# Routed experts and three convolution layers: VectorE's filter products, row normalisation and two start-up steps in another order

## The chip, the cores and the metric

One core of a Trainium2 chip runs the whole kernel in one launch. The metric is the device time in microseconds (us) of that core. A time is the median of several executions; the profile comes from one execution more.

## What is computed

The input x has 4 batches of 512 tokens with 512 channels (16 heads of 32). Four layers follow, each `x = x + layer(groupnorm(x))`. The first is a mixture of 8 experts with the best 2 per token; the other three are causal depthwise convolutions over the tokens with 3, 7 and 15 taps, mixed by a small matrix. Cut to what matters:

```
logits = x @ gate_w.T                      # groupnorm(x), 2048 tokens x 512
top_logit, top_idx = top_k(logits, 2);  gw = softmax(top_logit)
for e in range(8):
    we = sum(where(top_idx == e, gw, 0))
    out += we * ((silu(x @ w1[e].T) * (x @ w3[e].T)) @ w2[e].T)
...
y = concat([causal_dwconv(x, w) for w in (w3, w7, w15)])   # layers 1 to 3
out = einsum('blhm,dm->blhd', y, w_mix)
```

Everything is float32; a product is made of three passes (high by high, high by low, low by high) over a high part and a low part of each operand.

## The kernel before

The experts part takes about 745 us and the convolutions the rest. Gating and routing come first. Then the tokens stand in 35 blocks of 128 rows, sorted by expert, 4 or 5 blocks to each. For block g of expert e the engines do this:

- **GpSimd (POOL)** gathers the 128 rows of block g+1 from x into `block_row` by an indirect DMA (`fetch_rows`, L429 to L436), once TensorE has turned block g (`xT_done`), and then adds the finished rows of block g-2 into `acc` in DRAM by another (`add_block`, L438 to L446). It waits for that addition to land before it goes on. There is one `block_row`.
- **VectorE (DVE)** normalises the gathered rows (`normalise_rows`, L727), multiplies gate and up (`hidden`, L785), and makes the low parts: of x (`xT_low`, L768), of the turned hidden rows (`hT_low`, L773), of w1 and w3 (L733) and of w2 (L740).
- **ScalarE (ACT)** makes the high parts (w2: L517; hT: L534; filters: L524), SiLU (L552), and takes the finished, weighted rows out of PSUM (`y_row`, L540).
- **TensorE (PE)** runs in `body`: 48 matmuls for gate and up of block g (L934), the turn of block g+1 (`next_rows`, four transposes, L911), the down product of block g-1 (L921, L924), and eight transposes of hidden (L946).
- **SyncE (SP)** loads w1, w3 (`w13_raw`, 4 pieces) and w2 (2 halves) of the next expert as soon as their buffers are free, and then stores this expert's filters (L376), in this order in its queue.

While the experts run, VectorE also builds the block Toeplitz filters of the convolutions, one expert after the other, between the first and the second block of experts 1 to 7 (`after_first`): six products of taps and mixing matrix (L755), of which ScalarE takes the high part (L524) and VectorE the low part (L763). They lie in `filter_sb`, which is a piece of the tile `rows`, and go from there to DRAM. `filter_sb` is cleared once (L453), since the products fill only part of it; `filters_out` counts the stores, and the products of expert e wait until those of expert e-1 have landed.

The order of work on each engine is written out by hand. `all_blocks` (L332) sets it: for an expert, `new_expert`, `body` for its first block, `after_first`, and then `body` for each of the other blocks.

At the start, `place`, `weight_block` and other one-hot matrices of the routing borrow the tiles of w2. `at_block` lies in `w2_raw`, and VectorE's `expand_weights` is the last to read it; TensorE's `find_weights` (L902) reads `place` and `weight_block` in `w2_hi` and `w2_lo` and ends with `values_done`.

Of the kernel before, what the change touches and what calls it, by code (L numbers as in the profile page):

```python
# [11 lines left out]
TOP_K = 2  # L12
# [10 lines left out]
PARTS_OF_WEIGHT = 2  # L23
# [126 lines left out]
def wait_apart(eng, semaphore, value, counter):  # L150

    eng.wait_ge(semaphore, value)
    eng.sem_inc(counter, 1)


def experts_part(nc, x, gate_wT, w13T, w2T, acc, ident, group_mean, taps, mixT, filters, filters_out):
# [5 lines left out]
    with ExitStack() as ctx:  # L162
# [6 lines left out]
        def sem(name):  # L169
            return ctx.enter_context(nc.semaphore(name))  # L170
# [28 lines left out]
        filter_sb = late_rows[:, 0:4 * LAGS].rearrange("p (i s n) -> p i s n", i=2, s=2)  # L199
# [80 lines left out]
        weight_block_ok = sem("weight_block_ok")  # L280
        ids_done = sem("ids_done")
        lanes_done = sem("lanes_done")
        values_done = sem("values_done")
# [28 lines left out]
        filter_zero = sem("filter_zero")  # L312
# [6 lines left out]
        def load_w13(eng, e, k):  # L319
            eng.dma_start(w13_raw[:, k], w13T[bass.ds(e, 1), k].rearrange("o p t n -> (o p) t n"))\  # L320
               .then_inc(w13_in[k], 16)

        def load_w2(eng, e, half):
            k = slice(half * KF // 2, (half + 1) * KF // 2)
            eng.dma_start(w2_raw[:, k], w2T[bass.ds(e, 1), :, k].rearrange("o p t n -> (o p) t n"))\
               .then_inc(w2_in[half], 16)

        def last_block_of(eng, e):

            return eng.value_load(table[0:1, bass.ds(e, 1)], min_val=0, max_val=MAX_BLOCKS - 1)  # L330
# [17 lines left out]
        @block.sync  # L348
        def _(sp):
            for b in range(BATCH):  # L350
                sp.dma_start(rows[:, b * QUARTERS:(b + 1) * QUARTERS, 0:D], x_rows[b]).then_inc(x_in[b], 16)
            for k in range(KD):
                load_w13(sp, 0, k)

            sp.wait_ge(values_done, 1)
            for half in range(2):
                load_w2(sp, 0, half)


            sp.dma_start(taps_sb, taps).then_inc(taps_in, 16)  # L360
            sp.dma_start(mix_sb, mixT).then_inc(taps_in, 16)


            with sp.Fori(1, E) as e:
                for k in range(KD):
                    sp.wait_ge(w13_ok, (e - 1) * KD + k + 1)
                    if k >= 2:
                        sp.wait_ge(w13_in[k - 2], 16 * (e + 1))
                    load_w13(sp, e, k)
                for half in range(2):  # L370
                    sp.wait_ge(w2_ok, (e - 1) * 2 + half + 1)
                    sp.wait_ge(w13_in[KD - 2 + half], 16 * (e + 1))
                    load_w2(sp, e, half)
                for i in range(2):
                    wait_apart(sp, filter_ok, e * 2 + (i - 1), sp_passed)
                    sp.dma_start(filters[:, bass.ds(e * 8 + (4 * i - 8), P // HD)].rearrange("r a s n -> r a (s n)"),  # L376
                                 filter_sb[:, i].rearrange("p s n -> p (s n)")).then_inc(filters_out, 16)

        @block.gpsimd
        def _(pool):  # L380
# [48 lines left out]
            def fetch_rows(g):  # L429

                at = slice(g, g + 1) if isinstance(g, int) else bass.ds(g, 1)
                nc.gpsimd.tensor_copy(fetch[:, :], from_row[:, at]).then_inc(fetch_ok, 1)
                wait_apart(pool, fetch_ok, g + 1, passed)
                pool.indirect_dma_start(
                    out=block_row[:, :], out_offset=None, in_=x_by_row,
                    in_offset=bass.IndirectOffsetOnAxis(fetch[:, 0:1].bitcast(u32), 0)).then_inc(row_in, 16)  # L436
# [10 lines left out]

            pool.wait_ge(route_ok, 1)
            fetch_rows(0)
            pool.wait_ge(xT_done, 1)  # L450
            fetch_rows(1)
            pool.wait_ge(values_ok, 1)
            nc.gpsimd.memset(filter_sb, 0.0).then_inc(filter_zero, 1)  # L453
            pool.wait_ge(acc_ready, 32)
            pool.sem_inc(y_free, FREE)

# [9 lines left out]
            g = last_block_of(pool, E - 1)  # L466
# [100 lines left out]
        def _(dve):  # L567
# [148 lines left out]
            def take_weights():  # L716

                dve.wait_ge(values_done, 1)
                step(nc.vector.tensor_copy(row_value[:, 2, 1:1 + COLUMNS], y_ps[:, 0:COLUMNS]))
                nc.vector.tensor_tensor(row_value[:, 2, 1:1 + COLUMNS], row_value[:, 2, 1:1 + COLUMNS],  # L720
                                        y_ps[:, COLUMNS:2 * COLUMNS], ALU.add).then_inc(values_ok, 1)

            def normalise_rows(g):

                at = slice(g + 1, g + 2) if isinstance(g, int) else bass.ds(g + 1, 1)
                dve.wait_ge(row_in, 16 * (g + 1))
                nc.vector.tensor_scalar(block_row[:, :], block_row[:, :], row_value[:, 0, at], row_value[:, 1, at],  # L727
                                        ALU.subtract, ALU.mult).then_inc(row_ok, 1)
# [7 lines left out]
            def split_w2(e, g0):  # L736
                for half in range(2):
                    dve.wait_ge(w2_hi_ok, 2 * e + (half + 1))
                    k = slice(half * KF // 2, (half + 1) * KF // 2)
                    nc.vector.tensor_tensor(w2_lo[:, k], w2_raw[:, k], w2_hi[:, k].bitcast(f32),  # L740
                                            ALU.subtract).then_inc(w2_ok, 1)

            def after_first(e, g0):
                split_w2(e, g0)
                if isinstance(e, int):
                    dve.wait_ge(taps_in, 32)
                    dve.wait_ge(filter_zero, 1)
                    return
                dve.wait_ge(filters_out, e * 32 + (FILTERS_FREE - 32))
                for i in range(2):  # L750
                    c = bass.ds(e * 2 + (i - 2), 1)
                    tap = 0
                    for s, k in enumerate(SCALES):
                        at = SCALE_AT[s] + (QUARTERS - 1) * HD
                        last = nc.vector.tensor_tensor(  # L755
                            filter_sb[:, i, 1, at:at + k * HD].rearrange("p (k d) -> p k d", d=HD),
                            taps_sb[:, c, tap:tap + k].rearrange("p o k -> p (o k)")[:, :, None].to_broadcast([P, k, HD]),
                            mix_sb[:, c, s, :].to_broadcast([P, k, HD]), ALU.mult)
                        tap += k
                    last.then_inc(product_ok, 1)  # L760
                for i in range(2):
                    dve.wait_ge(filter_hi_ok, e * 2 + (i - 1))
                    nc.vector.tensor_tensor(filter_sb[:, i, 1].bitcast(f32r), filter_sb[:, i, 1], filter_sb[:, i, 0],  # L763
                                            ALU.subtract).then_inc(filter_ok, 1)

            def xT_low(g):
                dve.wait_ge(xT_hi_ok, g + 1)
                nc.vector.tensor_tensor(xT_lo[:, :, :].rearrange("p a n -> p (a n)"), xT_ps[:, :],  # L768
                                        xT_hi[:, :, :].rearrange("p a n -> p (a n)").bitcast(f32), ALU.subtract).then_inc(xT_ok, 1)

            def hT_low(g):
                dve.wait_ge(hT_hi_ok, g + 1)
                nc.vector.tensor_tensor(hT_lo[:, :, :], hT_ps[:, :, :], hT_hi[:, :, :].bitcast(f32),  # L773
                                        ALU.subtract).then_inc(hT_ok, 1)

            def body(e, g, first):
                if not isinstance(g, int):
                    hT_low(g - 1)
                if isinstance(g, int) or not first:
                    normalise_rows(g + 1)  # L780
                dve.wait_ge(silu_ok, g + 1)
                if not isinstance(g, int):

                    dve.wait_ge(hT_done, g)
                nc.vector.tensor_tensor(hidden[:, :].rearrange("p (a n) -> p a n", a=2),  # L785
                                        silu[:, :].rearrange("p (a n) -> p a n", a=2), up_ps[:, :, :],
                                        ALU.mult).then_inc(hidden_ok, 1)
                xT_low(g + 1)
                if isinstance(g, int):
                    take_weights()  # L790
# [15 lines left out]
            expand_weights()  # L806
            take_targets()
            all_blocks(dve, new_expert, body, after_first)
            hT_low(last_block_of(dve, E - 1))

# [684 lines left out]
```

## Time and profile before

| | |
|---|---|
| median of 3 runs | 1171.56 us (1164.51 to 1361.69) |
| profiled execution, device time | 1166.2 us |
| its span | 1164.3 us |
| TensorE matmuls busy | 1060.9 us (91%) |
| VectorE busy | 501.3 us (43%) |
| ScalarE busy | 318.5 us (27%) |
| GpSimd busy | 128.1 us (11%) |
| experts part in the span | 0 to about 745 us |

How to read it: busy shares are averages over stages. TensorE has work nearly all the time, so what matters is where it has none, and what ended each of those gaps. In the timeline a bracket behind a row gives the idle time of the engine ahead of it and the instruction that ended it; "PEclk" is the clock granted to TensorE, as a share of full speed. The device time is 1.9 us longer than the span, for what lies around it.

### The profile page before, as it was taken

Reading aid. Unit: us, or ns where it says so; the run is one execution under the profiler, and the core shown is the slowest. Engines: PE = TensorE matmul, PEld = TensorE weight load, DVE = VectorE, ACT = ScalarE, POOL = GpSimd, SP = SyncE. Lnnn points to the kernel's source line nnn. Section 1 sums busy time; section 2 is a strip of 40 time slices with the busy share of each in tenths; the row PEclk is TensorE's granted clock in tenths of the full one; section 3 lists DMA queues with packets and bytes.
Section 4 is the critical chain, followed back from the end, with each engine's and each line's share of the span. In section 5 each row is a group of like instructions: output and inputs, shape, how many; then the busy total and the mean of one; then the engine's idle time right before and its main releaser. Section 6 shows DMA issues by size and latency. Waiting matters only on the chain. (4 is left out here: it accounts for less than half of the span.)

```text
span 1164.3 us, 14374 instructions
## 1 busy us (share of the span) xinstructions
PE 1060.9 (91%) x5234; PEld 883.5 (76%) x5235; DVE 501.3 (43%) x692; ACT 318.5 (27%) x433; POOL 128.1 (11%) x170
## 2 busy tenths in 40 slices
PE   5588999999999999999999999168999979989998
PEld 3377887887887887887878877158888968888887
DVE  5773163154245263154451452135325952387011
ACT  2403242142243242153431432012301220122112
POOL 2013111211211212111212111000000000000000
PEclk9769999999999999999999999667999989999999
DMA  8208218316415519217338140492998299698993
GB/s 361 82 19 316 48 28 314 76 27 245 138 33 196 185 18 351 39 27 278 105 112 275 27 137 18 128 238 63 205 193 182 47 220 208 127 192 168 204 207 100
DMA packets 66336, 172.72 MB, mean 148 GB/s; under 512 B 8192, under 2 KB 38016, under 8 KB 57280
## 3 DMA queue, kind: packets, MB, share of 16 engines
q1 hardware_dynamic: 58080, 149.19, 45.1%
q0 software_dynamic: 8080, 23.07, 9.4%
q8 instruction: 21, 0.34, 0.1%
q14 instruction: 11, 0.09, 0.0%
q10 hardware_dynamic: 144, 0.02, 0.0%
HBM read 136.15 MB, written 40.30 MB: 152 GB/s over the span
## 5 line engine op out<-in xcount | busy, mean ns | idle before, releaser
L1409 PE MATMUL head_ps<-split,ring 128*128 128x512 f32 (+1 forms) x630 | 225.8, 358 | 18.7 <-DMA ring<-filters 17.2
L1413 PE MATMUL head_ps<-split,ring 128*128 128x512 f32 (+1 forms) x630 | 220.2, 350 | 0.0
L1410 PE MATMUL head_ps<-split,ring 128*128 128x512 f32 (+1 forms) x630 | 219.8, 349 | 0.0
L1409 PEld LDWEIGHTS head_ps<-split,ring 128*128 128x128 f32 x630 | 123.6, 196 | 35.2 <-DMA ring<-filters 17.8
L1413 PEld LDWEIGHTS head_ps<-split,ring 128*128 128x128 f32 x630 | 123.3, 196 | 15.7
L1410 PEld LDWEIGHTS head_ps<-split,ring 128*128 128x128 f32 x630 | 123.7, 196 | 14.9
L921 PE MATMUL y_ps<-w_hi,hT_hi 128*128 128x512 f32 x280 | 117.5, 420 | 1.2 <-ACT hT_hi L534 1.2
L785 DVE TENSOR_TENSOR hidden<-silu,up_ps 128x1024 f32<-128x1024 f32 x35 | 42.7, 1219 | 165.0 <-ACT silu L552 165.0
L921 PE MATMUL y_ps<-w_lo,hT_hi 128*128 128x512 f32 x280 | 113.5, 405 | 0.0
L1236 DVE TENSOR_TENSOR stream<-stream,head_ps 128x512 f32<-128x512 f32 (+1 forms) x63 | 34.1, 557 | 176.2 <-PE head_ps L1413 176.2
L773 DVE TENSOR_TENSOR hT_lo<-hT_ps,hT_hi 128x1024 fp32r<-128x1024 f32 x35 | 42.7, 1221 | 134.0 <-ACT hT_hi L534 134.0
L552 ACT ACTIVATE silu<-gate_ps 128x1024 f32<-128x1024 f32 x35 | 35.9, 1025 | 235.5 <-PE up_ps L934 235.5
L934 PE MATMUL gate_ps<-w_hi,xT_hi 128*128 128x512 f32 x280 | 89.9, 402 | 1.7 <-DVE xT_lo L768 1.7
L443 POOL DMA_INDIRECT acc<-y_row,put x35 | 63.4, 1810 | 214.6 <-ACT y_row L540 206.3
L934 PE MATMUL up_ps<-w_hi,xT_hi 128*128 128x512 f32 x280 | 86.9, 392 | 0.0
L934 PE MATMUL up_ps<-w_lo,xT_hi 128*128 128x512 f32 x280 | 86.8, 391 | 0.0
L934 PE MATMUL gate_ps<-w_lo,xT_hi 128*128 128x512 f32 x280 | 86.7, 391 | 0.0
L934 PE MATMUL gate_ps<-w_hi,xT_lo 128*128 128x512 f32 x280 | 86.6, 391 | 0.0
L934 PE MATMUL up_ps<-w_hi,xT_lo 128*128 128x512 f32 x280 | 86.3, 390 | 0.0
L733 DVE TENSOR_TENSOR w_lo<-w_raw,w_hi 128x2048 fp32r<-128x2048 f32 x32 | 71.9, 2285 | 4.7 <-ACT w_hi L509 4.7
L924 PE MATMUL y_ps<-w_hi,hT_lo 128*128 128x512 f32 x280 | 69.3, 389 | 0.0
L921 PEld LDWEIGHTS y_ps<-w_hi,hT_hi 128*128 128x128 f32 x280 | 55.7, 199 | 12.8 <-issue 1.4
(189 smaller groups left out, 1362.8 us busy)
## 6 DMA issues: line engine op xcount, KB each, us to landing
w_raw<-in_w13T SPq DMA_DIRECT2D x32, 1024.0 KB, 11.5
ring<-filters SPq DMA_DIRECT2D x60, 480.0 KB, 10.4
filters<-rows SPq DMA_DIRECT2D x14, 1568.0 KB, 7.2
w_raw<-in_w2T SPq DMA_DIRECT2D x16, 1024.0 KB, 6.1
ring<-filters SPq DMA_DIRECT2D x84, 192.0 KB, 6.2
ring<-filters SPq DMA_DIRECT2D x48, 288.0 KB, 7.2
rows<-in_x SPq DMA_DIRECT2D x4, 1024.0 KB, 8.1
rowed<-acc SPq DMA_DIRECT2D x4, 1024.0 KB, 12.1
```

Source lines behind the costliest of these rows:

```text
L443: pool.indirect_dma_start(out=acc[:, :], out_offset=bass.IndirectOffsetOnAxis(put[:, 0:1].bitcast(u32), 0), in_=y_row[:, :], in_offset=Non ...
L552: nc.scalar.activation(silu[:, :].rearrange("p (a n) -> p a n", a=2), gate_ps[:, :, :], ACT.Silu).then_inc(silu_ok, 1)
L733: nc.vector.tensor_tensor(w13_lo[:, k], w13_raw[:, k], w13_hi[:, k].bitcast(f32), ALU.subtract).then_inc(w13_ok, 1)
L773: nc.vector.tensor_tensor(hT_lo[:, :, :], hT_ps[:, :, :], hT_hi[:, :, :].bitcast(f32), ALU.subtract).then_inc(hT_ok, 1)
L785: nc.vector.tensor_tensor(hidden[:, :].rearrange("p (a n) -> p a n", a=2), silu[:, :].rearrange("p (a n) -> p a n", a=2), up_ps[:, :, :], ...
L921: nc.tensor.matmul(y_ps[:, :], hT_hi[:, k, :], b[:, k, :], start=(k == 0 and b is w2_hi), stop=False)
L924: last = nc.tensor.matmul(y_ps[:, :], hT_lo[:, k, :], w2_hi[:, k, :], start=False, stop=(k == KF - 1))
L934: last = nc.tensor.matmul(o[:, n, :], a[:, k, :], b[:, k, t, n * 512:(n + 1) * 512], start=(k == 0 and a is xT_hi and b is w13_hi), stop=( ...
L1236: nc.vector.tensor_tensor(x, x, head_ps[n % BANKS][:, columns(pair)], ALU.add).then_inc(summed, 1)
L1409: nc.tensor.matmul(place, kernel_hi, x_hi, start=(u == 0 and a == 0), stop=False)
L1410: nc.tensor.matmul(place, kernel_lo, x_hi, start=False, stop=False)
L1413: last = nc.tensor.matmul(place, kernel_hi, x_lo, start=False, stop=(u == len(units) - 1 and a == windows(s) - 1))
```

## The change

Four edits. On VectorE, in `after_first` of experts 1 to 7, the split of w2 moves from ahead of the six filter products to behind them; and in `body` of every block that isn't an expert's first, `normalise_rows(g + 1)` moves ahead of `hT_low(g - 1)`. On GpSimd the memset of `filter_sb` moves from behind the wait for `values_ok` to between the gathers of blocks 0 and 1. On SyncE the loads of w2 of expert 0 wait for `weight_block_ok` (4) in the place of `values_done`.

```diff
@@ SyncE
-            sp.wait_ge(values_done, 1)
+            sp.wait_ge(weight_block_ok, PARTS_OF_WEIGHT * TOP_K)
             for half in range(2):
                 load_w2(sp, 0, half)
@@ GpSimd
             fetch_rows(0)
+            nc.gpsimd.memset(filter_sb, 0.0).then_inc(filter_zero, 1)
             pool.wait_ge(xT_done, 1)
             fetch_rows(1)
             pool.wait_ge(values_ok, 1)
-            nc.gpsimd.memset(filter_sb, 0.0).then_inc(filter_zero, 1)
             pool.wait_ge(acc_ready, 32)
@@ VectorE, after_first
-                split_w2(e, g0)
                 if isinstance(e, int):
+                    split_w2(e, g0)
                     dve.wait_ge(taps_in, 32)
                     dve.wait_ge(filter_zero, 1)
                     return
...
                     last.then_inc(product_ok, 1)
+                split_w2(e, g0)
                 for i in range(2):
                     dve.wait_ge(filter_hi_ok, e * 2 + (i - 1))
@@ VectorE, body
+                if isinstance(g, int) or not first:
+                    normalise_rows(g + 1)
                 if not isinstance(g, int):
                     hT_low(g - 1)
-                if isinstance(g, int) or not first:
-                    normalise_rows(g + 1)
                 dve.wait_ge(silu_ok, g + 1)
```

The lines behind the change are numbered one higher in the changed kernel. The first place is VectorE between the first block of an expert and its second: `w2_lo` L740 is the first of the two halves in the split of w2, `rows` L755 a filter product, `rows` L763 a filter's low part. Before:

```order
L768 TENSOR_TENSOR xT_lo<-xT_ps,xT_hi 128x512
...
L740 TENSOR_TENSOR w2_lo<-w2_raw,w2_hi 128x2048
...
L755 TENSOR_TENSOR rows<-rows 128x96
...
L755 TENSOR_TENSOR rows<-rows 128x480
L763 TENSOR_TENSOR rows<-rows 128x1568 x2
...
L773 TENSOR_TENSOR hT_lo<-hT_ps,hT_hi 128x1024
...
L727 TENSOR_SCALAR block_row<-block_row,row_value 128x512
...
L785 TENSOR_TENSOR hidden<-silu,up_ps 128x1024
```

and now, at the same place:

```order
L769 TENSOR_TENSOR xT_lo<-xT_ps,xT_hi 128x512
...
L755 TENSOR_TENSOR rows<-rows 128x96
...
L755 TENSOR_TENSOR rows<-rows 128x480
...
L740 TENSOR_TENSOR w2_lo<-w2_raw,w2_hi 128x2048
...
L764 TENSOR_TENSOR rows<-rows 128x1568 x2
...
L727 TENSOR_SCALAR block_row<-block_row,row_value 128x512
L774 TENSOR_TENSOR hT_lo<-hT_ps,hT_hi 128x1024
...
L786 TENSOR_TENSOR hidden<-silu,up_ps 128x1024
```

The products now stand ahead of the two splits of w2, and `block_row` ahead of `hT_lo`. The second place is GpSimd at the start, where `rows` is the filter buffer. Before:

```order
L432 COPY fetch<-from_row 128x1 [waits route_ok]
L434 DMA block_row<-in_x,fetch 128x512 [waits fetch_ok]
L432 COPY fetch<-from_row 128x1 [waits xT_done]
L434 DMA block_row<-in_x,fetch 128x512 [waits fetch_ok]
L453 MEMSET rows 128x6272 [waits values_ok]
L330 TENSOR_LOAD table [waits acc_ready]
```

and now:

```order
L432 COPY fetch<-from_row 128x1 [waits route_ok]
L434 DMA block_row<-in_x,fetch 128x512 [waits fetch_ok]
L450 MEMSET rows 128x6272
L432 COPY fetch<-from_row 128x1 [waits xT_done]
L434 DMA block_row<-in_x,fetch 128x512 [waits fetch_ok]
L330 TENSOR_LOAD table [waits values_ok,acc_ready]
```

The memset has gone from ahead of the third gather to ahead of the second, and no longer waits.

## Rows read from the trace of the kernel before

**Rows 1.** Waits of TensorE from 95 to 740 us: us in total, times, longest.

```profile
PE xT_ps L911 <- DVE block_row L727: 20.4, 9, 2.9
```

**Rows 2.** Timeline of TensorE, the turns: start, us, what [idle ahead <-releaser].

```profile
105.77 0.47 PE L911 MATMUL xT_ps<-ident,block_row 128*128 128x128 f32 x1 [2.92 <-DVE block_row L727]
...
125.01 0.60 PE L911 MATMUL xT_ps<-ident,block_row 128*128 128x128 f32 x4
...
142.74 0.49 PE L911 MATMUL xT_ps<-ident,block_row 128*128 128x128 f32 x3
...
160.48 0.60 PE L911 MATMUL xT_ps<-ident,block_row 128*128 128x128 f32 x4
...
180.91 0.90 PE L911 MATMUL xT_ps<-ident,block_row 128*128 128x128 f32 x3 [2.54 <-DVE block_row L727]
...
291.75 0.44 PE L911 MATMUL xT_ps<-ident,block_row 128*128 128x128 f32 x2 [0.20 <-DVE block_row L727]
...
718.62 0.60 PE L911 MATMUL xT_ps<-ident,block_row 128*128 128x128 f32 x4
```

**Rows 3.** Timeline of VectorE, expert 1, 162 to 181 us.

```profile
162.87 0.68 DVE L768 TENSOR_TENSOR xT_lo<-xT_ps,xT_hi 128x512 fp32r<-128x512 f32 x1
168.55 4.50 DVE L740 TENSOR_TENSOR w_lo<-w_raw,w_hi 128x2048 fp32r<-128x2048 f32 x2 [5.00 <-ACT w_hi L517]
172.97 2.16 DVE L755 TENSOR_TENSOR rows<-rows 128x96 f32 x6
175.67 3.49 DVE L763 TENSOR_TENSOR rows<-rows 128x1568 fp32r<-128x1568 f32 x2 [0.54 <-ACT rows L524]
179.08 1.22 DVE L773 TENSOR_TENSOR hT_lo<-hT_ps,hT_hi 128x1024 fp32r<-128x1024 f32 x1
180.22 0.63 DVE L727 TENSOR_SCALAR block_row<-block_row,row_value 128x512 f32<-128x512 f32 x1
```

**Rows 4.** Timeline of ScalarE, expert 1, 166 to 178 us.

```profile
166.60 3.72 ACT L517 ACTIVATE w_hi<-w_raw 128x2048 fp32r<-128x2048 f32 x2 [4.42 <-PE y_ps L924]
174.12 2.92 ACT L524 ACTIVATE rows<-rows 128x1568 fp32r<-128x1568 f32 x2 [3.80 <-DVE rows L755]
176.95 0.67 ACT L540 ACTIVATE y_row<-y_ps,row_value 128x512 f32<-128x512 f32 x1
```

**Rows 5.** Stretches of TensorE: span, busy (instructions), PEclk, DMA share, GB/s.

```profile
178.00:184.00 6.00, 3.46 (x12) 0.72 0.88 362
271.00:277.00 6.00, 3.55 (x18) 1.00 0.89 368
```

**Rows 6.** Timeline of GpSimd, ScalarE and VectorE, expert 0, 91 to 106 us.

```profile
91.55 5.34 POOL L453 MEMSET rows<- 128x6272 f32 x1 [14.59 <-DVE row_value L720]
...
97.84 0.99 POOL L434 DMA_INDIRECT block_row<-in_x,fetch  x1 [0.83 <-POOL fetch L432]
...
96.15 1.92 ACT L517 ACTIVATE w_hi<-w_raw 128x2048 fp32r<-128x2048 f32 x1 [7.53 <-DMA w_raw<-in_w2T]
...
100.56 2.29 DVE L740 TENSOR_TENSOR w_lo<-w_raw,w_hi 128x2048 fp32r<-128x2048 f32 x1 [0.16 <-ACT w_hi L517]
...
105.17 0.55 DVE L727 TENSOR_SCALAR block_row<-block_row,row_value 128x512 f32<-128x512 f32 x1 [1.18 <-DMA block_row<-in_x,fetch]
```

**Rows 7.** Timeline of GpSimd and VectorE at the start, 64 to 77 us.

```profile
64.10 1.46 POOL L434 DMA_INDIRECT block_row<-in_x,fetch  x1 [0.93 <-POOL fetch L432]
...
74.16 2.80 POOL L434 DMA_INDIRECT block_row<-in_x,fetch  x1 [0.83 <-POOL fetch L432]
...
70.55 0.55 DVE L727 TENSOR_SCALAR block_row<-block_row,row_value 128x512 f32<-128x512 f32 x1
```

**Rows 8.** Timeline of GpSimd and VectorE, expert 1, 178 to 199 us.

```profile
178.44 2.19 POOL L443 DMA_INDIRECT acc<-y_row,put  x1 [14.98 <-ACT y_row L540]
192.53 1.00 POOL L434 DMA_INDIRECT block_row<-in_x,fetch  x1 [0.81 <-POOL fetch L432]
...
198.35 0.55 DVE L727 TENSOR_SCALAR block_row<-block_row,row_value 128x512 f32<-128x512 f32 x1 [4.35 <-DMA block_row<-in_x,fetch]
```

## The prediction

> **What bounds the kernel now.** I read TensorE's waits first, over the experts part from 95 to 740 us. One wait holds nearly all of TensorE's idle time there: the turn of the next block waits for the row normalisation, 20.4 us in 9 times [rows 1]. The timeline of the turns [rows 2] shows where. Between undisturbed blocks the turns stand 17.73 us apart (125.01 to 142.74, to 160.48). The turn at 180.91 comes 20.43 us after its forerunner, with 2.54 us of idle ahead of it: it is the second turn of expert 1. Seven experts have such a gap of 2.4 to 2.5 us, expert 0 one of 2.92 at 105.77, and one of 0.20 stands at 291.75.
>
> The gaps cost more than the idle time. After the gap in expert 1 TensorE ran at a granted clock of 0.72 over 178 to 184 us, against 1.00 over the same stretch of expert 2 [rows 5]: a mix of 1.2 and 2.4 GHz against 2.4 alone. So I take the whole cost from the turns and not from the waits: from 142.74 to 718.62 there are 31 blocks, 575.88 us; 31 times 17.73 are 549.63. The excess is 26.25 us, over seven experts 3.75 each, of which some 2.5 are the wait and the rest lost clock.
>
> Why is VectorE late there? Its timeline of expert 1 [rows 3] says it in one look. It stands idle for 5.00 us ahead of the split of w2, waiting for ScalarE's high part, which in turn waits for the down product of the block before (`w_hi` at 166.60, 4.42 idle) [rows 4]. Then VectorE does everything at once: split 168.55 to 173.05, products to 175.13, 0.54 idle for ScalarE's filter parts, low parts to 179.16, `hT_lo` to 180.30, and only then `block_row`, to 180.85. ScalarE meanwhile stands idle 3.80 us for the products [rows 4]. TensorE would have been ready for the turn at 160.48 + 17.73 = 178.21.
>
> **Products ahead of the split, experts 1 to 7.** The six products, 2.16 us, go into the 5.00 us of idle: 163.55 to 165.71. Their inputs are there, and their wait is for the stores of the expert before, issued two blocks of 17.73 us earlier or more. Behind them the split is queued, so a late store would hold w2's low part too; I cost that at nothing. ScalarE no longer waits: 166.60 + 3.72 = 170.32, filter parts to 173.24. VectorE: split 168.55 to 173.05 as before, low parts at once, to 176.54. The edit takes out 2.16 of products and 0.54 of waiting. w2's low part isn't later than before.
>
> **Rows ahead of hT's low part.** `block_row` then runs 176.54 to 177.17 in the place of 180.85: 3.68 us earlier, of which 1.1 are this edit. TensorE wants it at 178.21, so 1.04 us are left over and the gap closes. `hT_lo` follows, to 178.4. The down product wants it behind its first 16 matmuls, some 4 us after the turn; its high part on ScalarE is done by 175, since `y_row` (L540) and hT's high part follow the filter parts. In blocks without filters the order changes nothing, as VectorE has idle time on both sides. One new risk: `hT_lo` now stands behind a wait for the gather, and a late gather would hold it and then the down product.
>
> **What is late next.** `y_row` also comes 3.71 us earlier, at 173.24, and with it the addition into `acc`: 178.44 becomes 174.73. From there to the next gather it was 14.09 us, and from the gather to the normalisation 5.82 [rows 8]. With these lengths the third turn's rows are ready at 174.73 + 14.09 + 5.82 + 0.55 = 195.19, and TensorE wants them at 178.21 + 17.73 = 195.94. That leaves 0.75 us. It is thin, and the 0.20 at 291.75 is this same chain. The lengths are those of full queues: the filter stores and the next expert's weights start at the same moment. Now these start 2.6 us earlier and the addition 3.7 earlier, so it gets in front of them by one more us. I take no wait here, between a gain of nothing and the price of rival 1.
>
> **Start of expert 0.** The gap at 105.77 cost 2.92 us and 19.24 − 17.73 = 1.51 of clock behind it, 4.43 together. Two things were late [rows 6]. The gather of block 2 was issued at 97.84, behind the memset of 5.34 us; without that it is issued at about 92.5, and with the same 7.33 us to the normalisation its rows are there at 99.8. VectorE was busy with w2's split until 102.85, because ScalarE had waited 7.53 us for the load. With the load issued when `expand_weights` ends, some 9 us earlier, ScalarE starts when it may, at about 91.6, so the split ends near 98. TensorE wants the turn at 105.77 − 2.92 = 102.85. The rows are ready at 100.4, with over 2 us left. The whole 4.43 goes. Each of the two edits alone would leave a part of the gap. The SyncE edit pulls taps, mixing matrices and expert 1's weights forward too; nothing else is in the queues then but the gather, whose 7.33 us were already those of full queues.
>
> The memset's new place is the one price I see. It begins when the first gather is issued, at 65.56, and ends at 70.90; the first normalisation, on which TensorE waits, began at 70.55 [rows 7]. Nothing in the trace shows a memset beside that instruction. From below the cost is nothing, as the two work on different tiles. From above: the second gather's issue took 2.80 us here against 0.99 later, so GpSimd is stretched by up to 1.8 us beside VectorE's splits; a memset stretched so would end at 72.7 and could hold the normalisation for 2.2 us. I take 0.35, the distance from 70.55 to 70.90. The second gather may be issued up to 2 us later; TensorE wants its rows only behind the 48 matmuls of block 0.
>
> By the Trainium skill (SBUF — State Buffer, "SBUF: two separate sides") VectorE in a two-port mode and GpSimd hold a shared pair of ports exclusively, for a whole instruction, so whichever starts first blocks the other. By that rule the normalisation would be held to the end of the memset; if it doesn't bind here, the sum is 0.35 lower. The 2.80 us issue beside the splits agrees with it, as far as one row can.
>
> **Sum.** The profiled execution took 1166.2 us. 1166.2 − 26.25 − 4.43 + 0.35 = 1135.9, say 1136. That execution lies between the lowest run and the median (1164.51, 1171.56), so the runs of the changed kernel may lie 2 us below or 6 above this. The convolutions keep their work and their own gaps, which start from DMAs.
>
> **Rivals.**
> 1. The third turn waits instead. If the chain from addition to rows doesn't shorten and each expert is late by about 1 us, it pays this and up to 1.5 us of clock: 7 × 2.5 = 17.5, 1153; with half of that 1145. For it: the margin of 0.75. Against it: the addition now goes ahead of the stores.
> 2. The gap shrinks but stays, because VectorE or ScalarE lose the 1.04 us of margin elsewhere (the filter low parts start on the second filter's high part, ready at 173.24 against 173.05). 0.5 us of wait and 1.3 of clock in seven experts are 12.6: 1148.
> 3. Slower: stores and weights that start earlier fill the queues just when the addition's rows are written, and the chain of rows 8 grows. With a lateness x at the third turn an expert pays x + 1.5 us; it breaks even with the kernel before at x = 2.9 (7 × 4.4 = 31), where the chain of 19.9 us has grown by 3.7. If it grows by 9, x is 8.2 and the time 1136 + 68 = 1204; by 5, 1176. Against it: the same traffic was there before at nearly the same moment, and gave 14.09.
> 4. The change does nothing in experts 1 to 7, as something other than VectorE ends the wait. Then only expert 0's part is left, 1162. Against it: rows 3 show no wait for the gather ahead of `block_row` at 180.22.
>
> **How the numbers follow.** Forecast 0.67, rival 1 0.13, rival 2 0.11, rival 3 0.04, rival 4 0.02, the rest spread around. About 2% is what a measurement here can tell from no change; from 1166.2 that is below 1143, from the median below 1148. The forecast lies beyond it almost always, and rivals 1 and 2 in a part of their cases: faster 0.77, within 2% 0.19, slower 0.04. The range goes from 1130 (forecast without the memset's cost, on a fast run, and a little of the convolutions' clock) to 1150 (rivals 1 and 2 at their middle).
>
> **What would show it.** In the profile after: turns 17.7 us apart throughout; TensorE's wait for `block_row` from 95 to 740 us near 0 in place of 20.4; VectorE's wait for `w_hi` shorter by 2.2 us an expert, ScalarE's wait for the products gone; `acc` additions some 3.7 us earlier in each expert; the convolutions begin near 715 us. Wrong would be: waits at the third turn, a lower clock in the experts without a gap, or a first turn later than 71.5 us.

## The result, and the profile after

The changed kernel took 1137.25 us (median of 4 runs, 1132.44 to 1140.69), against 1168.34 us for the kernel before (median of 4 runs); the ratio is 0.974, 95% interval 0.972 to 0.976. One of the four executions of the kernel before took 1361.69 us, and the ratio leaves it out. Forecast were 1136 us, in a range from 1130 to 1150. The profiled execution took 1132.44 us with a span of 1130.7, 33.6 us shorter than that of before.

The answer to [rows 1], TensorE's waits for `block_row` in the changed kernel (us in total, times, longest):

```profile
PE xT_ps L912 <- DVE block_row L727: 0.4, 1, 0.4
```

20.4 us in nine waits have become 0.4 in one. The turns, TensorE's timeline, as in [rows 2]:

```profile
102.80 0.44 PE L912 MATMUL xT_ps<-ident,block_row 128*128 128x128 f32 x2 [0.39 <-DVE block_row L727]
...
120.55 0.60 PE L912 MATMUL xT_ps<-ident,block_row 128*128 128x128 f32 x4
...
138.25 0.60 PE L912 MATMUL xT_ps<-ident,block_row 128*128 128x128 f32 x4
...
155.94 0.60 PE L912 MATMUL xT_ps<-ident,block_row 128*128 128x128 f32 x4
173.63 0.60 PE L912 MATMUL xT_ps<-ident,block_row 128*128 128x128 f32 x4
...
191.33 0.60 PE L912 MATMUL xT_ps<-ident,block_row 128*128 128x128 f32 x4
...
686.74 0.60 PE L912 MATMUL xT_ps<-ident,block_row 128*128 128x128 f32 x4
```

The second turn of expert 1, at 173.63, now comes 17.69 us behind its forerunner, as all 31 do: 138.25 to 686.74 are 548.49 us, where it was 575.88 before. VectorE's timeline of expert 1, the answer to [rows 3]:

```profile
158.34 0.68 DVE L769 TENSOR_TENSOR xT_lo<-xT_ps,xT_hi 128x512 fp32r<-128x512 f32 x1
158.94 2.16 DVE L755 TENSOR_TENSOR rows<-rows 128x96 f32 x6
164.01 4.49 DVE L740 TENSOR_TENSOR w_lo<-w_raw,w_hi 128x2048 fp32r<-128x2048 f32 x2 [2.91 <-ACT w_hi L517]
168.42 3.48 DVE L764 TENSOR_TENSOR rows<-rows 128x1568 fp32r<-128x1568 f32 x2
171.82 0.54 DVE L727 TENSOR_SCALAR block_row<-block_row,row_value 128x512 f32<-128x512 f32 x1
172.28 1.22 DVE L774 TENSOR_TENSOR hT_lo<-hT_ps,hT_hi 128x1024 fp32r<-128x1024 f32 x1
```

The products fill the idle time ahead of the split, of which 2.91 us are left. `block_row` ends at 172.36, 1.27 us before TensorE wants it. ScalarE [rows 4] no longer waits for products:

```profile
162.06 3.72 ACT L517 ACTIVATE w_hi<-w_raw 128x2048 fp32r<-128x2048 f32 x2 [4.40 <-PE y_ps L925]
165.68 2.90 ACT L524 ACTIVATE rows<-rows 128x1568 fp32r<-128x1568 f32 x2
168.49 0.67 ACT L540 ACTIVATE y_row<-y_ps,row_value 128x512 f32<-128x512 f32 x1
```

TensorE around that turn, the answer to [rows 5] (stretch, length, busy, PEclk, DMA share, GB/s), is busy throughout, at 2.4 GHz:

```profile
171.00:177.00 6.00, 6.00 (x30) 1.00 0.89 298
```

The chain from the addition into `acc` to the rows of the third turn, as in [rows 8], on GpSimd and VectorE:

```profile
169.98 1.69 POOL L443 DMA_INDIRECT acc<-y_row,put  x1 [11.05 <-ACT y_row L540]
...
180.91 1.00 POOL L434 DMA_INDIRECT block_row<-in_x,fetch  x1 [0.81 <-POOL fetch L432]
...
187.97 0.55 DVE L727 TENSOR_SCALAR block_row<-block_row,row_value 128x512 f32<-128x512 f32 x1 [11.25 <-DMA block_row<-in_x,fetch]
```

From addition to gather it is 10.93 us now and was 14.09; from gather to normalisation 7.06, and it was 5.82. The third turn, at 191.33, has 2.81 us in hand. At last the start, as in [rows 6] and [rows 7], on GpSimd, ScalarE and VectorE:

```profile
65.30 5.33 POOL L450 MEMSET rows<- 128x6272 f32 x1
...
93.40 2.77 POOL L434 DMA_INDIRECT block_row<-in_x,fetch  x1 [0.83 <-POOL fetch L432]
...
91.08 3.72 ACT L517 ACTIVATE w_hi<-w_raw 128x2048 fp32r<-128x2048 f32 x2 [2.90 <-DVE row_value L720]
...
70.27 0.65 DVE L727 TENSOR_SCALAR block_row<-block_row,row_value 128x512 f32<-128x512 f32 x1
...
93.03 4.50 DVE L740 TENSOR_TENSOR w_lo<-w_raw,w_hi 128x2048 fp32r<-128x2048 f32 x2 [1.98 <-ACT w_hi L517]
102.19 0.55 DVE L727 TENSOR_SCALAR block_row<-block_row,row_value 128x512 f32<-128x512 f32 x1 [4.67 <-DMA block_row<-in_x,fetch]
```

The split of w2 ends at 97.53 as forecast, but the third gather's issue takes 2.77 us in the place of 0.99, and its rows come only at 102.19.

So the 33.6 us come from three stretches of the span: 27.39 between the turns of blocks 4 and 35; 4.49 ahead of them (142.74 against 138.25); and 1.72 behind them (445.68 against 443.96), in the end of the experts and the convolutions, which the change doesn't touch.

### The profile page after: what moved, and what is told of

Its sections match the earlier page's. It is cut to its first block and busy times, and to the rows that moved or that the text cites. A ratio compares the mean times of both kernels' runs of the same rounds, so it can differ in the third digit from the quotient of the medians.

```text
span 1130.7 us, 14347 instructions
## 1 busy us (share of the span) xinstructions
PE 1045.8 (92%) x5234; PEld 874.1 (77%) x5235; DVE 500.0 (44%) x692; ACT 318.3 (28%) x433; POOL 127.5 (11%) x170
## 5 line engine op out<-in xcount | busy, mean ns | idle before, releaser
L1410 PEld LDWEIGHTS head_ps<-split,ring 128*128 128x128 f32 x630 | 122.3, 194 | 34.5 <-DMA ring<-filters 17.2
L1414 PEld LDWEIGHTS head_ps<-split,ring 128*128 128x128 f32 x630 | 122.0, 194 | 15.9 <-DVE split L1228 0.2
L1411 PEld LDWEIGHTS head_ps<-split,ring 128*128 128x128 f32 x630 | 122.4, 194 | 14.9
L922 PE MATMUL y_ps<-w_hi,hT_hi 128*128 128x512 f32 x280 | 112.7, 402 | 1.2 <-ACT hT_hi L534 1.2
L922 PE MATMUL y_ps<-w_lo,hT_hi 128*128 128x512 f32 x280 | 109.2, 390 | 0.0
L443 POOL DMA_INDIRECT acc<-y_row,put x35 | 61.0, 1742 | 208.2 <-ACT y_row L540 201.8
L727 DVE TENSOR_SCALAR block_row<-block_row,row_value 128x512 f32<-128x512 f32 x36 | 19.7, 548 | 130.9 <-DMA block_row<-in_x,fetch 130.9
L922 PEld LDWEIGHTS y_ps<-w_hi,hT_hi 128*128 128x128 f32 x280 | 52.6, 188 | 11.7 <-issue 1.4
```

Of the source, the lines that this page charges most:

```text
L443: pool.indirect_dma_start(out=acc[:, :], out_offset=bass.IndirectOffsetOnAxis(put[:, 0:1].bitcast(u32), 0), in_=y_row[:, :], in_offset=Non ...
L922: nc.tensor.matmul(y_ps[:, :], hT_hi[:, k, :], b[:, k, :], start=(k == 0 and b is w2_hi), stop=False)
L1410: nc.tensor.matmul(place, kernel_hi, x_hi, start=(u == 0 and a == 0), stop=False)
L1411: nc.tensor.matmul(place, kernel_lo, x_hi, start=False, stop=False)
L1414: last = nc.tensor.matmul(place, kernel_hi, x_lo, start=False, stop=(u == len(units) - 1 and a == windows(s) - 1))
```

## The experiments

The theory: VectorE's order of work sets the gap at the second turn of each expert, and each gap costs its wait and some clock. Rivals: the edits don't add up, work at that place always costs, or something other than the wait set the clock.

### The four parts

`products_only` has only the move of the products on VectorE:

```diff
@@ VectorE, after_first
-                split_w2(e, g0)
                 if isinstance(e, int):
+                    split_w2(e, g0)
...
                     last.then_inc(product_ok, 1)
+                split_w2(e, g0)
```

> VectorE's queue theory: the products alone take 2.7 us out ahead of block_row. The changed kernel had 1.27 us in hand at the second turn, and the rows edit is worth 1.13 of it, so 0.1 stays in hand: no gap or one under 0.2 us in experts 1 to 7, expert 0 keeps its gap of 2.9. Time 26 us below the kernel before, ratio 0.977; if small gaps of 0.2 stay and each costs clock, 0.985. Rival (the gap closes only with both edits): gaps of 1 us and more, ratio 0.99 or above.

Measured: 1139.95 us, ratio 0.978 (0.975 to 0.982). No gap in experts 1 to 7; `block_row` and the second turn of expert 1 in its trace:

```profile
177.09 0.53 DVE L727 TENSOR_SCALAR block_row<-block_row,row_value 128x512 f32<-128x512 f32 x1
...
177.80 0.60 PE L912 MATMUL xT_ps<-ident,block_row 128*128 128x128 f32 x4
```

It is ready 0.18 us ahead. The products alone are enough, and barely so.

`rows_only` has only `normalise_rows` ahead of `hT_low`:

```diff
@@ VectorE, body
+                if isinstance(g, int) or not first:
+                    normalise_rows(g + 1)
                 if not isinstance(g, int):
                     hT_low(g - 1)
-                if isinstance(g, int) or not first:
-                    normalise_rows(g + 1)
```

> VectorE's queue theory: block_row comes 1.13 us earlier, so the gap in experts 1 to 7 shrinks from 2.5 to about 1.4 us. If the lost clock behind it stays (some 1.3 us), 8 us below the kernel before, ratio 0.993. If a gap of 1.4 us no longer takes the clock down, 7 x 2.4 = 17 us below, ratio 0.985. Rival (the order of these two doesn't matter): 1.000.

Measured: 1157.71 us, ratio 0.992 (0.990 to 0.995). The time is that of the first case, for another reason. TensorE's waits and the two turns of expert 1:

```profile
PE xT_ps L911 <- DVE block_row L727: 19.1, 14, 3.0
```

```profile
180.27 0.66 PE L911 MATMUL xT_ps<-ident,block_row 128*128 128x128 f32 x4 [1.34 <-DVE block_row L727]
199.13 0.66 PE L911 MATMUL xT_ps<-ident,block_row 128*128 128x128 f32 x4 [0.94 <-DVE block_row L727]
```

The gap is 1.34 us long, as expected, and takes no clock: over 178 to 184 us the granted clock is 1.00. But now the third turn waits too, by 0.80 to 1.63 us in six of the seven experts, again at a granted clock of 1.00. ScalarE still stands waiting for the products, so `y_row` and the addition are as late as before, with 14.0 us from addition to gather, while TensorE comes earlier. This is the mechanism of the prediction's first rival: with the products left where they were, the chain to the third turn is as long as before, and that turn waits.

`no_start` has both VectorE edits and neither start-up edit.

> Both VectorE edits, neither start-up edit: the seven gaps go, that of expert 0 (2.9 us and 1.5 of clock) stays. 26 to 28 us below the kernel before, ratio 0.977. If the parts weren't additive (the start-up edits mattered for the later experts), 0.98 or above.

Measured: 1137.71 us, ratio 0.977 (0.973 to 0.981). One wait for `block_row` is left from 95 us on, 2.9 us, that of expert 0; the 31 periods take 548.50 us.

`start_only` has the two start-up edits alone:

```diff
@@ SyncE
-            sp.wait_ge(values_done, 1)
+            sp.wait_ge(weight_block_ok, PARTS_OF_WEIGHT * TOP_K)
@@ GpSimd
             fetch_rows(0)
+            nc.gpsimd.memset(filter_sb, 0.0).then_inc(filter_zero, 1)
...
             pool.wait_ge(values_ok, 1)
-            nc.gpsimd.memset(filter_sb, 0.0).then_inc(filter_zero, 1)
```

> The two start-up edits without VectorE's: expert 0's gap shrinks from 2.9 us to 0.4 or less if the gather of block 2 sets it. But in the old order hT_lo stands ahead of block_row, which costs nothing here, as hT's high part is there by 96. 4.0 us below the kernel before, ratio 0.9965; seven gaps of 2.5 us stay.

Measured: 1163.83 us, ratio 0.998 (0.9965 to 0.9998), some 2.5 us less than the kernel before where 4.0 were expected. The gap shrinks to 1.16 us and not to 0.4; the seven others stay. The third gather's issue again takes 2.77 us and its rows come at 104.04, 9.6 us after it began.

`memset_only` and `w2load_only` split these two again, for a look at the trace.

> Only the memset moved. The third gather is issued at about 92.5 in the place of 97.8, but VectorE splits w2 until 102.8 since the load of w2 is as late as before: block_row at 104.0 to 104.5 (hT_lo stands ahead of it), gap of expert 0 about 1.7 us in the place of 2.9. Rival (the gather alone sets the gap): the gap goes to 0.4. The first block_row takes 0.65 in the place of 0.55 us and isn't held to the end of the memset.

Measured: 1166.91 us in one run. The gap is 1.9 us. The gather is issued at 94.75 and takes 0.98, and VectorE reaches `block_row` at 105.04, behind the split (to 103.99) and `hT_lo`. As expected, the split sets it.

> Only the load of w2 moved. VectorE's split ends near 98, but the third gather stands behind the memset, issued at 97.8: its rows are there at 105 again or, if the queues are emptier by then, at 103 to 104. Gap of expert 0 between 1.0 and 2.9 us. Rival (the split alone sets the gap): no gap.

Measured: 1167.60 us in one run. The gap is 2.7 us, and GpSimd's timeline shows why:

```profile
92.54 5.38 POOL L453 MEMSET rows<- 128x6272 f32 x1 [14.95 <-DVE row_value L720]
97.84 1.16 POOL L432 COPY fetch<-from_row 128x1 int32 x1
99.83 0.98 POOL L434 DMA_INDIRECT block_row<-in_x,fetch  x1 [0.83 <-POOL fetch L432]
```

Each edit alone leaves most of the gap: after one of them the other's lateness sets it. The device times of these two can't be told from the kernel before's.

### How much is in hand

`late_small` is the changed kernel with one product on VectorE more, whose result isn't used, behind the filters' low parts in experts 1 to 7:

```diff
+        spare = [sb(f"spare{n}", [P, WIDE]) for n in range(1)]   # WIDE = 640
...
                                             ALU.subtract).then_inc(filter_ok, 1)
+                for s in spare:
+                    some = late_rows[:, mix_at:mix_at + WIDE]
+                    nc.vector.tensor_tensor(s[:, :], some, some, ALU.mult)
```

> The changed kernel with one more VectorE product of 128x640 (about 0.8 us, its result is not used) behind the low parts of the filters in experts 1 to 7. 1.27 us were in hand at the second turn, so 0.4 stay in hand: no gap, ratio to the kernel before as for the change, 0.974. Rival (work added on VectorE there always costs, or the wait is set elsewhere): 7 x 0.8 = 6 us more, 0.979.

Measured: 1136.39 us, ratio 0.974 (0.971 to 0.977). 0.8 us of work more on VectorE, seven times, cost nothing; 0.53 us stay in hand at the second turn.

`late_big2` has two sums over 1280 columns there. Two products of that width (`late_big`) find no room for their results in SBUF, and gave no time; a sum writes one column.

```diff
+                some = late_rows[:, mix_at:mix_at + 1280].rearrange("p (a n) -> p a n", a=1)
+                for n in range(2):
+                    nc.vector.tensor_reduce(spare[:, n:n + 1], some, axis=AX.X, op=ALU.add)
```

> The changed kernel with two VectorE sums over 128x1280 (about 2.8 us together, results not used) behind the low parts of the filters in experts 1 to 7. 1.27 us are in hand at the second turn, so a gap of 1.5 us opens there in experts 1 to 7. The products-in-hand account: with 1.0 to 1.5 us of lost clock behind each gap 7 x 2.5 to 3.0 = 18 to 21 us above the changed kernel, ratio to the kernel before 0.990 to 0.992. If gaps this short take no clock: 7 x 1.5 = 11 us, 0.983. The third turn keeps over 1 us in hand, since the addition into acc is as early as in the changed kernel.

Measured: 1147.07 us, ratio 0.984 (0.982 to 0.986). TensorE's waits, and the stretch around the gap of expert 1:

```profile
PE xT_ps L916 <- DVE block_row L728: 10.9, 8, 1.4
```

```profile
176.00:182.00 6.00, 4.59 (x23) 1.00 1.02 336
```

In experts 1 to 7 the period up to the second turn is 19.26 us and the next one 17.76, against 17.69 twice: 1.64 us lost, of which 1.41 are the recorded wait. The granted clock behind the gap is 1.00 in all seven. The second branch of the expectation holds.

`late_more` has a third such sum, over 960 columns, so that the gap is as long as it was in the kernel before.

> The changed kernel with three VectorE sums over 128x1280, 1280 and 960 (about 4.0 us together, results not used) behind the low parts of the filters in experts 1 to 7: the gap at the second turn is then 2.7 us, as long as in the kernel before, while with 2.87 us of sums it was 1.4 and took no clock. If the length of the gap decides about the clock: part of the experts lose 1.2 to 1.6 us more behind it as in the kernel before, 7 x 2.7 and 5 x 1.5 = 26 us above the changed kernel, ratio to the kernel before 0.995 to 1.000. If the clock loss of the kernel before had another cause (its late addition, ScalarE's idle time), 7 x 2.7 = 19 us, 0.991. The third turn keeps over 2 us in hand either way.

Measured: 1163.54 us, ratio 0.997 (0.995 to 0.998). Waits and the stretch:

```profile
PE xT_ps L916 <- DVE block_row L728: 18.2, 8, 2.5
```

```profile
176.00:186.00 10.00, 8.04 (x33) 0.83 1.03 368
```

Six of seven experts lose 1.4 to 1.7 us of clock behind the gap. The 31 periods take 577.02 us, against 575.88 in the kernel before. So 4 us of work put on VectorE at this one place, seven times, give back the whole gain of the experts. What the gap costs depends on its length: with 1.4 us of idle none of 7 lost clock, with 2.5 us 11 of 14 did (5 of 7 in the kernel before).

The other traces say the same. From 95 us on they have, with these, 27 waits for `block_row` of 0.39 to 1.63 us, and none lost clock; of 35 of 2.44 to 2.57 us 27 did, and of 5 of 2.74 to 2.98 us all. Expert 0's gap in `memset_only`, 1.89 us ahead of 105.63, lies between. TensorE around it:

```profile
103.00:109.00 6.00, 4.11 (x16) 0.80 0.99 385
```

The period behind it is 19.36 us, so it lost clock. Why 8 of the 35 long ones lost none is not shown.

### What shortened the chain to the third turn

`loads_first` is the changed kernel with the loads of the next expert's w1 and w3 ahead of the filter stores in SyncE's queue:

```diff
-            with sp.Fori(1, E) as e:
-                for k in range(KD):
-                    sp.wait_ge(w13_ok, (e - 1) * KD + k + 1)
...
+            next_w13(1)
+            next_w2(1)
+            with sp.Fori(1, E - 1) as e:
+                next_w13(e + 1)
+                store(e)
+                next_w2(e + 1)
+            with sp.Fori(E - 1, E) as e:
+                store(e)
```

> The changed kernel with the loads of the next expert's w1 and w3 ahead of the filter stores in SyncE's queue, so that they run some 20 us earlier and are through before the addition into acc that follows the filters. If it is the load traffic that makes that addition slow (10.9 us from its issue to the next gather's in the changed kernel, 14.1 before), it takes 9 us or less, and the third turn has more than the 2.7 us in hand it has now. If the lag comes from something else (GpSimd's own issue, the addition's place in its queue), it stays at 10.9. The time stays that of the changed kernel, 0.974, as no wait is left there to remove; 1 us more would mean that the early loads slow the gather of the second turn.

Measured: 1134.84 us, ratio 0.974 (0.971 to 0.976). GpSimd in expert 1:

```profile
171.31 1.69 POOL L456 DMA_INDIRECT acc<-y_row,put  x1 [7.82 <-ACT y_row L553]
...
182.22 1.00 POOL L447 DMA_INDIRECT block_row<-in_x,fetch  x1 [0.82 <-POOL fetch L445]
```

It is 10.91 us again, the second branch of the expectation. But the run doesn't empty the queues. In the changed kernel SyncE issued the stores from 170.47 on, the loads of w1 and w3 from 173.28 and those of w2 from 191.96. In `loads_first` it was:

```profile
145.69 8.10 SPq L320 DMA_DIRECT2D w_raw<-in_w13T  x4
171.80 2.25 SPq L380 DMA_DIRECT2D filters<-rows  x2
174.37 2.49 SPq L325 DMA_DIRECT2D w_raw<-in_w2T  x2
```

An expert's filter stores stand ahead of the next expert's loads in this queue, and not behind them, as the description of the kernel before has it. With w1 and w3 out of the way the loads of w2 move up, and from 177 to 183 us the queues still carry 337 GB/s. So the run doesn't show by itself what the addition waits behind. Expert 7 says more, for which there is nothing more to load. GpSimd in expert 7, kernel before:

```profile
679.18 2.40 POOL L443 DMA_INDIRECT acc<-y_row,put  x1 [14.96 <-ACT y_row L540]
...
691.13 1.01 POOL L434 DMA_INDIRECT block_row<-in_x,fetch  x1 [0.83 <-POOL fetch L432]
```

and changed kernel:

```profile
647.70 1.71 POOL L443 DMA_INDIRECT acc<-y_row,put  x1 [11.05 <-ACT y_row L540]
658.09 1.00 POOL L434 DMA_INDIRECT block_row<-in_x,fetch  x1 [0.83 <-POOL fetch L432]
```

Without loads it was 11.95 us before, with them 14.1 to 14.4. After it is 10.39 without them and 10.4 to 10.9 with them. The other traces agree: 11.9 to 12.0 and 14.0 to 14.4 wherever the products stand behind the split, 10.3 to 10.9 with or without loads wherever they stand ahead of it, `products_only` too. So the move of the products alone shortened the chain, and of the 3.2 us some 2 are what the loads cost in the old place. The rest has 0.5 to 0.7 of the addition's own issue in it (1.69 us against 2.19 to 2.41). In the kernel before the first store was issued at 177.73, the addition at 178.44 and the loads from 180.55; in the changed kernel the addition comes first, at 169.98. That its place ahead of the others in the queues gives the gain is argued from this order and not shown.

`third_gather` is the changed kernel with the gather of block 2 ahead of GpSimd's waits:

```diff
             fetch_rows(1)
+            pool.wait_ge(xT_done, 2)
+            fetch_rows(2)
             pool.wait_ge(values_ok, 1)
...
-                pool.wait_ge(xT_done, g + 1)
-                fetch_rows(g + 1)
                 with pool.If(g > 1):
+                    pool.wait_ge(xT_done, g + 1)
+                    fetch_rows(g + 1)
                     add_block(g - 2)
```

> The changed kernel with the gather of block 2 ahead of GpSimd's waits for values_ok and acc_ready. It is issued at about 88.5 in the place of 93.4, when VectorE isn't splitting w2, so its issue takes 1.0 us in the place of 2.8 and the rows are there by 97. The last 0.4 us of waiting at expert 0 go; 0.4 us less than the changed kernel, which timing can't tell, but the trace can. If the late rows come from full queues alone, the issue still takes over 2 us.

Measured: 1136.50 us, ratio 0.975 (0.973 to 0.977).

```profile
90.15 0.98 POOL L434 DMA_INDIRECT block_row<-in_x,fetch  x1 [0.81 <-POOL fetch L432]
```

The issue takes 0.98 us when VectorE isn't splitting w2, and the last wait for `block_row` is gone. As expected, the time doesn't show it.

`after_again` is the changed kernel beside the last three.

> The changed kernel once more, beside the other three on one chip: ratio to the kernel before 0.974. No gap in experts 1 to 7, third turn 2.1 to 2.8 us in hand, 10.9 us from addition to gather.

Measured: 1134.92 us, ratio 0.975 (0.972 to 0.978). Neither `third_gather` nor `loads_first` beats it by what can be measured. Its one wait for `block_row` was 0.9 us.

## Why the prediction was right

**What bounds it.** Right. The waits for `block_row` were the whole of it, and the cost read from the turns, 26.25 us, was the right size: 27.39 went. The 1.1 more come from the steady period: 17.73 us was taken for all 31 blocks, where parts of the trace of before have 17.69, and the changed kernel has 17.69 throughout.

**The clock.** "So I take the whole cost from the turns and not from the waits" was the step that made the size right: the waits of the seven gaps alone are 17.3 us, where 27.4 went. Only, rival 2 charged a wait of 0.5 us with 1.3 us of clock, and rival 1 one of 1 us with 1.5. `late_big2` and `rows_only` show that such gaps took none. Both rivals were priced too high.

**Products ahead of the split.** Right in each time: ScalarE through with the filters 3.9 us earlier against TensorE's turns (3.8 forecast), products inside the idle, the split not later. `products_only` gives 26 of the 31 us.

**Rows ahead of hT's low part.** Forecast were 1.04 us in hand, measured 1.27. This edit isn't needed for the gap; it makes 1.27 us of reserve out of 0.18. The risk named with it, `hT_lo` behind a late gather, did not come up.

**What is late next.** The mechanism was right: `rows_only`, which leaves the addition late, ran into the third turn in six of seven experts. The size was off: with 0.75 us in hand forecast there were 2.1 to 2.8, since "with these lengths" took over 14.09 us for a chain that then took 10.9. The next step, from gather to normalisation, took 7.06 us where 5.82 were taken over, and gave 1.2 of it back. That the addition would get in front had been named, and not its size.

**Start of expert 0.** "The whole 4.43 goes" was off by a little: 4.0 went, and 0.39 us of wait stayed (0.9 in a second profile, 1.16 in `start_only`). The step that failed is "with the same 7.33 us to the normalisation": it was 8.79, as the gather's issue was stretched to 2.77 us under the split of w2, which the SyncE edit had pulled to that very place. The clock behind the gap came back, as the gap was short. "Each of the two edits alone would leave a part of the gap" holds: 1.9 and 2.7 us.

**The memset.** Taken at 0.35 us, it cost 0.10: the first `block_row` takes 0.65 us in all eight kernels with the early memset, and 0.55 in the four others and the kernel before. It began at 70.27, near the end of the memset (65.30 to 70.63), and ended at 70.92. Had all of it been held to the memset's end, it would have ended at 71.17 or later. The rule of the Trainium skill (SBUF — State Buffer, "SBUF: two separate sides"), that the later of the two is blocked for the whole instruction, is neither borne out nor refuted by this: 0.29 us of the normalisation lie behind the memset, and a hold of its second part alone would look the same. All eight kernels have the two at the same distance, so they are one case and not eight.

**The stretched issue.** The prediction took the 2.80 us of the second gather as a stretch "beside VectorE's splits". The traces have more to say: it is a matter of which comes first. VectorE's split of w2 in the kernel before and in the changed one, with the gathers at 97.84 (0.99 us) and 93.40 (2.77 us):

```profile
98.11 2.29 DVE L740 TENSOR_TENSOR w_lo<-w_raw,w_hi 128x2048 fp32r<-128x2048 f32 x1 [6.62 <-ACT w_hi L517]
```

```profile
93.03 2.29 DVE L740 TENSOR_TENSOR w_lo<-w_raw,w_hi 128x2048 fp32r<-128x2048 f32 x1 [1.98 <-ACT w_hi L517]
```

Issued 0.2 to 0.4 us ahead of the subtraction the gather took 0.98 or 0.99 us, in four traces. Issued 0.34 to 0.38 us behind its start it took 2.77 to 2.80 us, in 21 of 21 cases, and ended 0.85 to 0.88 us behind that subtraction's end, as if most of the issue had been held until then. The longer issues of the addition fit: in expert 1 of both kernels it ended 1.47 us behind the subtraction that was running (L763 to 179.16, L764 to 170.20), and the difference of 2.19 and 1.69 us is how much of that was left. The section of the Trainium skill just named has this as a second case, a VectorE instruction with two inputs in SBUF against a GpSimd instruction that reads SBUF; that the issue reads SBUF is not shown here, and the rows agree with the rule in one direction only: the subtraction that began under a gather's issue took 2.29 us, as the others did.

**The rest.** 1.72 us came from behind the last turn, forecast at nothing. Most of it is clock once more. In the last convolution TensorE waits for the filters; its wait and the stretch behind it, before and after:

```profile
1043.04 0.39 PE L1409 MATMUL head_ps<-split,ring 128*128 128x256 f32 x1 [3.42 <-DMA ring<-filters]
1043.00:1049.00 6.00, 5.96 (x37) 0.72 1.05 218
```

```profile
1010.95 0.39 PE L1410 MATMUL head_ps<-split,ring 128*128 128x256 f32 x1 [2.87 <-DMA ring<-filters]
1011.00:1017.00 6.00, 6.00 (x50) 1.00 1.05 218
```

Six of the fourteen profiles lost clock there, and the stretch behind the last turn is 444.6 to 445.7 us in them and 442.7 to 444.9 in the others. Five of the six lack one VectorE edit or both, and the sixth is `loads_first`; `rows_only` lost none. Whether the change has a part in this is open. Without it the profiled executions are 32.0 us apart, where 30.3 were forecast; the medians are 31.1 apart.

## What to carry to other kernels

An engine that is busy 43% of the time can still set every gap of the one that bounds the kernel: look at what stands in its queue ahead of the one result that is waited for, and move work that needs nothing into the idle time ahead of it. Price such a gap by the distance of the regular starts on both sides of it and not by the wait alone, since a longer gap also took clock and a shorter one didn't. When an engine that waits is freed, follow what it hands on: here the freed ScalarE brought the addition forward, and in `rows_only`, where it wasn't freed, part of the gain turned into a wait one block later.

## What was not expected

- The same gap costs one price at one length and another at another: 1.4 us of idle took no clock in 7 of 7 experts, 2.5 us took 1.4 to 1.7 us more in 11 of 14. The one gap between, of 1.89 us at expert 0, took clock too.
- An indirect DMA's issue on GpSimd took 0.98 us alone or just ahead of VectorE's subtraction of two SBUF tiles, and 2.77 to 2.80 when that subtraction had begun first. A short start-up wait hung on that.
- The steady period of a block is 17.69 us in some profiles (the changed kernel, `no_start`) and 17.73 in others (`third_gather`, parts of `products_only` and of the kernel before), 1.2 us over 31 blocks. Nothing that I looked at explains it.
